# Second expert matmul of an attention and expert layer in three rounded terms, its Gelu rows split a block ahead

## The reference

```python
# x: (16, 512, 128); 16 heads of 8; blocks of 64 rows; 4 experts of 512, the best 2 count
x = x + attention(layernorm(x))       # block sparse
x = x + experts(layernorm(x))

# attention: scores of block means choose one block of keys a head and block of queries, beside its own
c = einsum('bhmd,bhnd->bhmn', qb, kb) * SCALE
block_mask = (c >= top_k(c, 1)) | eye(M)
out = softmax(where(block_mask, q @ k.T * SCALE, -inf)) @ v
out = out @ proj_w.T + proj_b

# experts
h = gelu(einsum('nd,edh->enh', xf, w1) + b1, approximate=False)
y = einsum('enh,ehd->end', h, w2) + b2
out = einsum('nk,nkd->nd', gates, y_sel - c_sel + c_sum)
```

## Time and profile before

| | |
|---|---|
| median of 3 runs | 963.51 us (962.06 to 964.46) |
| profiled execution, its time | 965.21 us |
| profiled execution, its span | 963.5 us |
| mean granted TensorE clock | 0.973 |
| down matmuls (L400), busy | 242.2 us in y_ps, 14.5 us in v_ps |
| Gelu (L945) | 256, 689 ns each |
| exponential (L909) | 128, 1026 ns each |
| block maxima (L658) | 256, 691 ns each |
| sums of experts on GpSimd (L1045) | 48, 1287 ns each |

### The profile page before, as it was taken

The page is one execution under the profiler, slowest core; times in us unless marked ns, Lnnn a source line. Parts: engine busy times, 40 slices in busy tenths (PEclk is TensorE's granted clock), DMA queues, the critical chain, the costliest instruction groups (busy, mean ns, idle before and its releaser), DMA issues.

```text
span 963.5 us, 24241 instructions
## 1 busy us (share of the span) xinstructions
PE 908.3 (94%) x9638; PEld 607.0 (63%) x9638; DVE 555.1 (58%) x1552; ACT 460.0 (48%) x740; POOL 182.7 (19%) x183
## 2 busy tenths in 40 slices
PE   3898999999999999999999999999999999999995
PEld 3576666666657666666666666666666666666662
DVE  7545637475574747566574756657474755736321
ACT  1432373645537363553637364463736446373741
POOL 5601010212122121212112121212112121210211
PEclk8795899999999999999999999999999999999998
DMA  7440341615335251524426062533516153350110
GB/s 209 128 117 17 101 142 52 172 36 148 102 113 141 74 162 26 167 81 127 127 76 170 15 187 62 144 109 82 172 29 184 45 146 96 83 159 2 56 55 13
DMA packets 96020, 99.49 MB, mean 103 GB/s; under 512 B 8968, under 2 KB 82704, under 8 KB 95888
## 3 DMA queue, kind: packets, MB, share of 16 engines
q1 hardware_dynamic: 93168, 85.19, 31.3%
q0 software_dynamic: 2544, 12.58, 4.2%
q10 hardware_dynamic: 192, 0.13, 0.1%
HBM read 48.20 MB, written 28.71 MB: 80 GB/s over the span
## 4 chain that ended last, share of the span: by engine, by line
PE 63%; DVE 16%; issue 10%; ACT 4%; DMA 3%; SPq 2%; POOL 1%; DVEq 0%; POOLq 0%; ACTq 0%
PE y_ps L400 14%; PE s_ps L309 7%; PE s_ps L332 5%; PE o_ps L343 5%; PE s_ps L258 5%; DVE rmax L658 5%; PE s_ps L260 4%; PE s_ps L259 4%; ACT hid L945 3%; PE v_ps L318 2%; PE a_ps L373 2%; SPq L1116 2%; PE a_ps L267 2%; PE o_ps L350 2%; DVE nmax L667 2%
## 5 line engine op out<-in xcount | busy, mean ns | idle before, releaser
L400 PE MATMUL y_ps<-hid,w2s 128*128 128x512 f32 x480 | 242.2, 604 | 0.0
L909 ACT ACTIVATE prob<-s_ps 128x1024 f32<-128x1024 f32 x128 | 131.3, 1026 | 217.4 <-PE s_ps L332 217.4
L658 DVE TRANSPOSE_TENSOR_REDUCE rmax<-s_ps 128x16 bf16<-128x512 f32 x256 | 167.3, 691 | 58.5 <-PE s_ps L309 58.2
L945 ACT ACTIVATE hid<-s_ps,b1s 128x512 f32<-128x512 f32 x256 | 171.2, 689 | 35.2 <-PE s_ps L260 34.9
L309 PE MATMUL s_ps<-qdiag,kv 64*128 64x512 f32 x768 | 135.2, 458 | 5.5 <-DMA qdiag<-qpair 3.2
L667 DVE TENSOR_REDUCE nmax<-v_ps 16x64 bf16<-16x256 bf16 x128 | 52.3, 408 | 106.3 <-PE v_ps L325 106.2
L258 PE MATMUL s_ps<-xnhi,w1hi 128*128 128x512 f32 x256 | 111.5, 436 | 1.5
L1045 POOL TENSOR_TENSOR yT<-yT,gate_cols 128x512 f32<-128x512 f32 x48 | 61.8, 1287 | 269.8 <-DVE gate_cols L754 269.3
L309 PEld LDWEIGHTS s_ps<-qdiag,kv 64*128 64x128 f32 x768 | 85.4, 254 | 33.4 <-ACT hid L945 10.6
L902 ACT COPY vaug<-v_ps 128x128 f32<-128x128 f32 x128 | 34.1, 266 | 150.0 <-PE v_ps L318 149.3
L332 PEld LDWEIGHTS s_ps<-nmax,hone 16*128 16x128 bf16 x2048 | 67.5, 94 | 54.2 <-DVE nmax L667 27.9
(11 more groups left out here) (148 smaller groups left out, 1114.2 us busy)
## 6 DMA issues: line engine op xcount, KB each, us to landing
gate_cols<-gates SPq DMA_DIRECT2D x64, 256.0 KB, 5.1
kv_table<-stage SPq DMA_DIRECT2D x16, 768.0 KB, 3.9
kv<-stage SPq DMA_DIRECT2D x16, 768.0 KB, 6.3
kv_chosen<-selected SPq DMA_DIRECT2D x15, 768.0 KB, 5.3
kv<-kv_chosen SPq DMA_DIRECT2D x15, 768.0 KB, 4.9
qdiag<-qpair SPq DMA_DIRECT2D x504, 16.0 KB
xs<-in_x SPq DMA_DIRECT2D x16, 256.0 KB, 4.4
out_x<-x SPq DMA_DIRECT2D x16, 256.0 KB, 4.7
```

Of the source, the lines that this page charges most:

```text
L400: ins = pe.matmul(dst[:], w2s[:, n, :], hid[:, n, :], start=(c == 0), stop=(c == C - 1))
L658: v.tensor_reduce(rmax[m % 2][:, half * 8:(half + 1) * 8, :], s_ps[m % 2][:, half * N:(half + 1) * N].rearrange("p (a c) -> p a c", c=32), ...
L909: act.activation(prob[m % 2][:].rearrange("p h s -> p (h s)"), s_ps[m % 2][:], ACT.Exp, scale=SCALE).then_inc(exped, 1)
L945: act.activation(hid[:, k, :], up_ps[up_bank(k)], ACT.Gelu, bias=b1s[:, k:k + 1]).then_inc(gelued, 1)
```

## The change

- The down matmul takes three terms in place of one: `w2hi` x `hlo`, `w2lo` x `hhi`, `w2hi` x `hhi`, all float32r.
- The row of hid is split for it. ScalarE copies it to a high half `hhi` (`high`), and GpSimd subtracts that from the row to give the low half `hlo` (`low`). Both halves live in rings of three tiles. `high` of a chunk waits until TensorE has used the high half three chunks before, `low` likewise.
- High halves of block b - 2 are made in the steps of block b: chunks 2m + 2 and 2m + 3 in step m, after the exponential and attT and ahead of the values copy; chunks 0 and 1 during the up matmuls of the block before, ahead of the copy of attT. GpSimd's low halves stand in the same steps; the addition of projb and, in step 6, the gather move behind lows, and the sums in steps 4 and 6 stand ahead of them.
- In the tail VectorE makes the low halves of the odd chunks, GpSimd those of the even ones.
- `w2` lands in rows of hid and is split by GpSimd in block 1; the landing of wqkv moves into hid as well.
- One `stage` tile in place of two; the writers wait for the DMAs of the block before.
- The Gelu that overwrites a row of hid waits for its low half, and no longer for the whole expert's down matmuls.

```diff
@@ tensor: c_down
-                pe.wait_ge(gelued, UPS * b + n + 1)
-                ins = pe.matmul(dst[:], w2s[:, n, :], hid[:, n, :], start=(c == 0), stop=(c == C - 1))
+                if b == 0 and n == 0:
+                    pe.wait_ge(w2_split, E)
+                pe.wait_ge(*low_of(b, n))
+                i = chunk(b, n) % NS
+                pe.matmul(dst[:], w2hi[:, n, :], hlo[i][:], start=(c == 0), stop=False).then_inc(low_used, 1)
+                pe.matmul(dst[:], w2lo[:, n, :], hhi[i][:], start=False, stop=False)
+                ins = pe.matmul(dst[:], w2hi[:, n, :], hhi[i][:], start=False, stop=(c == C - 1))
@@ vector: a_k (and the same in scalar: a_v)
-                if b >= 2:
-                    v.wait_ge(table_out[j], 16 * times(b - 2, 2))
-                    v.wait_ge(own_in[j], 16 * times(b - 2, 2))
+                if b >= 1:
+                    v.wait_ge(table_out[1 - j], 16 * times(b - 1, 2))
+                    v.wait_ge(own_in[1 - j], 16 * times(b - 1, 2))
@@ vector, the tail
+            low(b - 1, 3)
             c_split(b)
+            low(b - 1, 5)
             c_gated(b - 1, 0)
             c_route(b)
+            low(b - 1, 7)
             ranked = c_logits(b)
...
@@ scalar
+            def high(b, n):
+                u = chunk(b, n)
+                act.wait_ge(gelued, u + 1)
+                if u >= NS:
...
+                        act.wait_ge(high_used, (u - NS) // C * (C - 1) + (u - NS) % C + 1)
+                act.copy(hhi[u % NS][:], hid[:, n, :]).then_inc(high_done, 1)
@@ scalar, the steps
                     if m in (3, 5, 7):
                         o_columns(b, (m - 3) // 2)
+                    if b >= 2 and m + 1 < M:
+                        high(b - 2, 2 * m + 2)
+                        high(b - 2, 2 * m + 3)
                     if m + 1 < M:
                         values(b, m + 1)
@@ scalar, the Gelus
                         c_up(b - 1, k)
+                    if b >= 1 and k in (2, 3):
+                        high(b - 1, k - 2)
                     if k == 3:
                         o_columns(b, T - 1)
@@ scalar, the tail
+            for n in range(2, 2 * C):
+                high(B - 2, n)
             c_logits(B - 1)
-            for k in range(UPS):
-                c_up(B - 1, k)
+            for e in range(E):
+                for k in range(e * C, (e + 1) * C):
+                    c_up(B - 1, k)
+                if e < 2:
+                    for n in range((e + 2) * C, (e + 3) * C):
+                        high(B - 2, n)
+                if e == 2:
+                    for n in range(C):
+                        high(B - 1, n)
+            for n in range(C, UPS):
+                high(B - 1, n)
@@ gpsimd
+            def low(b, n):
+                u = chunk(b, n)
+                g.wait_ge(high_done, u + 1)
+                if u >= NS:
+                    g.wait_ge(low_used, u - NS + 1)
+                g.tensor_tensor(hlo[u % NS][:], hid[:, n, :], hhi[u % NS][:].bitcast(F32), ALU.subtract).then_inc(low_done, 1)
@@ gpsimd, the steps
-                        if b >= 1 and m == 1:
+                        if b == 1 and m == 1:
                             a_rows(b + 1)
-                        if m == stages(b)[3] + 1:
+                        if b < 2 and m == stages(b)[3] + 1:
                             a_select(b + 1)
                     if b == 0 and m < E:
                         split_w1(m)
+                    if b == 1 and 1 <= m <= E:
+                        split_w2(m - 1)
+                    if b >= 2 and m in (4, 6):
+                        c_sum(b - 2, m // 2 - 1)
+                    if b >= 2 and m + 1 < M:
+                        low(b - 2, 2 * m + 2)
+                        if b + 1 < B and m == stages(b)[3] + 1:
+                            a_select(b + 1)
+                        low(b - 2, 2 * m + 3)
+                    if b >= 2 and b + 1 < B and m == 1:
+                        a_rows(b + 1)
                     if b >= 1 and m == 5:
                         c_split(b - 1)
-                    if b >= 2 and m in (4, 6):
-                        c_sum(b - 2, m // 2 - 1)
```

More of the change, by code:

```diff
@@ L95, in layer @@
         mT = sb("mT", [P, E])
-        NX, N2, NG = 3, 3, E
+        NX, N2, NG, NS = 3, 3, E, 3
         xs = [sb(f"xs{i}", [P, T, D]) for i in range(NX)]
@@ L108, in layer @@
         qdiag = [sb(f"qdiag{g}", [P, 2, HH, N // 2], F32R) for g in range(2)]
-        stage = [sb(f"stage{i}", [P, M, BS, 3], F32R) for i in range(2)]
+        stage = sb("stage", [P, M, BS, 3], F32R)
         kv = [sb(f"kv{i}", [P, M, KEYS, 3], F32R) for i in range(2)]
@@ L152, in layer @@
         yT = sb("yT", [P, N])
+        hhi = [sb(f"hhi{i}", [P, N], F32R) for i in range(NS)]
+        hlo = [sb(f"hlo{i}", [P, N], F32R) for i in range(NS)]
         tiemax, tieall = sb("tiemax", [P, 1]), sb("tieall", [1, 1])
@@ L160, in layer @@
         w1_landing = hid[:, 0:E, :]
+        w2_landing = hid[:, 2 * E:3 * E, :].rearrange("p e (c d) -> p (e c) d", d=D)
+        wqkv = hid[:, 3 * E + 1, 0:3 * D]
         b2s, cexp, mexp = (hid[0:E, 3 * E, n * D:(n + 1) * D] for n in range(3))
@@ L223, in up_before, with chunk, on_vector, low_of @@
             return next((i for i in reversed(range(k)) if up_bank(i) == up_bank(k)), None)
+        def chunk(b, n):
+            return UPS * b + n
+        def on_vector(b, n):
+            return n % 2 == 1 and (b == B - 1 or b == B - 2 and n >= 2)
+        def low_of(b, n):
+            u = chunk(b, n)
+            late = sum(on_vector(*divmod(i, UPS)) for i in range(UPS * (B - 2), u + 1))
+            return (low_done_tail, late) if on_vector(b, n) else (low_done, u + 1 - late)
         def times(b, ring):
@@ L1070, in pool @@
                         split_w1(m)
+                    if b == 1 and 1 <= m <= E:
[9 more added lines that the diff above has]
+                        a_rows(b + 1)
                     if b >= 1 and m == 5:
                         c_split(b - 1)
-                    if b >= 2 and m in (4, 6):
-                        c_sum(b - 2, m // 2 - 1)
                 if b >= 2:
                     c_sum(b - 2, E - 1)
+                if b >= 1:
+                    low(b - 1, 0)
+                    low(b - 1, 1)
                 inverse(b, mv2, veps2, rstd2, mean2_done, rstd2_done)
             b = B - 1
+            low(b - 1, 2)
             c_split(b)
-            for e in range(1, E):
-                c_sum(b - 1, e)
-            for e in range(1, E):
-                c_sum(b, e)
+            for n in (4, 6):
+                low(b - 1, n)
+            for n in (8, 10):
+                low(b - 1, n)
+            c_sum(b - 1, 1)
+            for n in (12, 14):
+                low(b - 1, n)
+            c_sum(b - 1, 2)
+            c_sum(b - 1, 3)
+            for n in (0, 2, 4, 6, 8):
+                low(b, n)
+            c_sum(b, 1)
+            for n in (10, 12):
+                low(b, n)
+            c_sum(b, 2)
+            low(b, 14)
+            c_sum(b, 3)
         def sync(s):
```

80 lines of the change are left out of this document (57 added, 23 removed).

## The result

The changed kernel takes **1029.2 us** (median; 1026.4 to 1033.2) against 964.0 us of the kernel before on the same chip: ratio **1.067**, 95% interval 1.061 to 1.073. That is 65 us slower. The prediction was 1035.5 us, range 938 to 1080.

A forecast was written before the change was run, and what follows sets the result against it. TensorE, busy 94% of the span, was taken as the bound, with two stretches already VectorE's. Blocks +44, +1.3 and +1, attT +11 and tail +16, less 1 of gain, gave +72 us on 963.5: 1035.5 us, range 938 to 1080.

The forecast's parts named there:

- TensorE's gain: Down matmuls: ceiling 2.6 us a block, at most 1.3 can arrive; 1 us in all booked.
- Steps 0 to 5: Blocked VectorE operations cost +0.5 (step 2), +0.7 (step 3), +0.1 (step 5) a block; step 0's copies cancel downs' gain.
- Step 6: GpSimd blocks crow, cties and crank, so TensorE's values transpose waits for the x add: +2.1 us a block (0 to 4).
- attT: Two high copies ahead of the attT copy stall the projection: +0.7 us a block, 15 blocks, +11 us.
- Nothing is added: Step 6: the gather goes out about 2.5 us later, but the next scores are 3 us later too; no cost.
- Block: Steps 2 to 6 together +3.4 us for blocks 2 to 14, +44 us; attT's 0.7 a block comes on top.
- Block 15: Last block, without index and query work: +1.3 us, besides attT's 0.7.
- The clock: Rival: the clock falls each block after step 6's stall, 2 to 4 us more a block, 1075 us; chance 0.08.
- The tail: After the last blocks' ups, downs wait for high and low halves, 2.7 us a group: +16 us (8 to 24).
- The staging tile: One staging tile in place of two: its readers finish some 40 us before the next writing, so no cost.
- Port kept between operations in line: Rival: VectorE waits through successive GpSimd operations, +6.4 us a block in 13 blocks, 1078 us; chance 0.17.
- two stretches of VectorE: 486.2 to 495.6 and 501.6 to 506.3 us: VectorE works without idle time, so a shorter TensorE gains nothing inside.

The follow-up runs named there:

- no_split: The changed kernel without both halves of the Gelu rows, the three terms multiplying one fixed tile; 948.5 us beside 961.9 before, ratio 0.983.
- att_first: The changed kernel with ScalarE's first two high copies in the ups moved behind the attT copy; 1022.7 us, ratio 1.066 to before.
- tail_plain: The changed kernel with plain float32 down products in the last two blocks; 1001.7 us, ratio 1.046 to before.
- before_order: The kernel before with only GpSimd's queue reordered: xnlo behind the gather, step 4's sum after the gate; 947.6 us, ratio 0.984.
- select_first: The changed kernel with GpSimd's gather ahead of the sum and both subtractions of step 6; 1037.6 us, ratio 1.080 to before.
- low_memset: The changed kernel with two GpSimd memsets of the same row in place of each GpSimd low-half subtraction; 1019.3 us, ratio 1.057 to before.
- sum_last: The changed kernel with GpSimd's step 6 in the order gather, low 14, low 15, sum; 1011.6 us, ratio 1.054 to before.
- five_edits: The changed kernel with att_first, tail_plain and GpSimd's step 6 ordered gather, low 14, low 15, xnlo, sum; 965.9 us, ratio 1.004 to before.
- eight_edits: five_edits plus projb's addition ahead of low 4 and 5, step 0's values copy ahead of high copies, low 9 after the gate; 951.6 us, ratio 0.984.
- no_low: The changed kernel without the low halves, the first term multiplying the high half instead; 966.7 us beside 961.9 before, ratio 1.003.

## Why the prediction was right, and where it was wrong

The direction and the mechanism were right, and the total was 6 us off; but its terms were off by more, to both sides, so that the total came this close is in part luck. Too high was the price of the blocks and too low that of the tail, and a clock that the sum had left to a rival made up for some of the difference.

- **TensorE's gain.** Ceiling of 2.6 us a block: measured, 54.5 to 51.9 us. What arrives was put at 1.3 us a block at most, and less 1 us in all was booked. no_split has 0.9 us a block and 5 us in the tail, 13.4 us, and that with one more operation blocked in step 6 (cties). This term was mis-sized by 12 us. The likely reason is that the losses of steps 0 to 5 were counted against a TensorE as slow as before (next item).
- **Steps 0 to 5.** Forecast +0.5, +0.7 and +0.1 a block, with the copies of step 0 taking what the downs there give. The operations were blocked as told (level 1.0 us, in step 3 gexp 0.5 and gate 0.7, the cast 0.9). By ScalarE's Exps in order of time, counted from the first of the block, the changed block stands at 15.12 us in step 3 against 15.04 before, at 20.52 against 20.22 in step 4 and at 31.02 against 30.79 in step 6: 0.2 to 0.3 in place of 1.3. The losses are real (no_split stands at 29.81 in step 6), but a good part of them was paid out of the gain.
- **Step 6.** Forecast +2.1, measured about +1.4 (38.32 against 36.66 at the Exp of step 7, less the 0.2 from before). The mechanism was right and one GpSimd operation too long: cties was blocked by xnlo and crank by the sum, where the forecast had the sum and low 14. Of the check that it named, an idle of TensorE of 2 to 3 us released by the x add, the trace has 2.28 us.
- **attT.** Forecast a stall of 0.7 us; measured 0.66 us at the projection, counted from the Exp of step 7, of which 0.49 is TensorE's idle time just before it; att_first gives the 0.66 back. One copy took 0.62 us, where 0.57 was taken. "Nothing is added" for the gather held nearly in the changed kernel (1.4 us of waits for the keys against 1.5 before), but with no reserve: att_first shows 7.5 us of waits for it as soon as the block gets shorter.
- **Block.** All this is 2.3 us, where 4.1 (3.4 and 0.7) were forecast. Block 15 took 0.9 us more (53.2 against 52.3), where 2.0 (1.3 and 0.7) were forecast.
- **The clock.** It was a rival of its own with 0.08. It came in part: the granted clock fell in four of the blocks, one of them 61.6, one 61.5 and two 59 us long, together some 10 us over the undisturbed length. That hid a part of the block's overestimate.
- **The tail.** Forecast +16 us (8 to 24), measured +22.5, and tail_plain gives 21.7 of them back. The wait of 2.7 us after a group of ups was met to the digit (2.72). Mis-sized was how often: nine waits for GpSimd's halves, 17.9 us, and two for VectorE's, 1.6 us, where three groups were counted with 2.9 us each and some more at the start and the end. A small part went through the clock, 0.89 over the tail in place of 0.94.
- **The staging tile**: nothing, as forecast.
- **Port kept between operations in line**: refuted for the steady block. The cast of 581.73 began in low 12 and ended at 582.73; it got in ahead of low 13, which began at 582.41 and then took 1.46 us. crow, cties and crank got in likewise, each behind one operation. At the start of the program one row normalisation did wait through two memsets in line (3.55 us, before and after the change); what makes the difference wasn't tried.

What failed beyond single terms was the comparison. The prediction read two stretches of VectorE in front of two stalls of 0.25 and 0.37 us, and gate and crow blocked in them. It used this only to tell where TensorE's gain dies. before_order shows that those two operations, blocked 0.6 us each, cost 1.3 us a block: the rows carried a change better than the one forecast. The idle times of 0.25 and 0.37 us had priced them at half of that.

## What to carry over

Before GpSimd is given new work, list what VectorE has in the chain at that time, and place the new operations around it. Here a queue's order was worth more than the arithmetic: from 964 to 948 us without the change, and with it from 1029 to 952, some 22 us of which are the plain products in the tail. An operation moved in an in-order queue has two prices, what it holds back beside it and what it holds back behind it: select_first freed the one and paid the other. And measure a gain on the kernel before with the same disorder removed, or the order is taken for the change.

## What the runs showed that was not expected

- A GpSimd memset didn't keep out VectorE's operations with two SBUF operands (gexp 0.16 us inside one, crow 0.23 us beside one), but it did keep out the one-operand cast (0.82 in place of 0.42 us) and was itself kept out by it (0.80 in place of 0.53 us).
- The granted clock doesn't simply follow the stall of step 6. Counted are the blocks with a mean below 1.00, of the fourteen behind the first. low_memset has a stall of 2.03 us there in every block, and its clock fell in ten; the changed kernel has 2.28 us and four, sum_last 1.3 us and two, five_edits and eight_edits 0.82 us and none. But select_first, with 1.3 us there and 1.2 us more at a down, has eight, and no_split (1.19 us), no_low (0.97 us) and before_order (no such stall) have two, one and one. What else decides it wasn't tried.
- A wait added to GpSimd's queue on the kernel's critical comparisons made the kernel faster, in both kernels in which it was made along with other moves; by itself it wasn't measured.
